# The V projection behind the G loop, and the PV matmuls of windowed attention one step later

## The reference

```
x1 = layernorm(x)
g = x1 @ Wg.T + bg ;  v = x1 @ Wv.T + bv          # 16 heads of 64
corr = g g^T / (|g_i| |g_j|), masked to j in [i-128, i]
corr = (corr + 1) / 2
denom = mean_j(corr) + 0.5
fit = 1 / (denom * sum_i(1 / denom))
attn = softmax_j(corr * fit, masked)
x = x + (attn @ v) @ Wo.T + bo
h = relu(layernorm(x) @ W_fc.T)^2 ; y = h @ W_proj.T
x = x + (spikes of y over 5 steps) / 5
```

## Time and profile before

| | us |
|---|---|
| median of 2 runs | 1728.33 (1723.23 to 1733.42) |
| the profiled execution | 1727.19 |
| its span on core 0, the slowest | 1726.2 |
| spans of the other cores | 1710.9 to 1723.3 |

### The profile page before, as it was taken

One profiled execution on the slowest core, in us unless ns is written; L12 is line 12 of the kernel. 1 busy time (PEld: TensorE's weight loads), 2 busy tenths in 40 slices (PEclk: granted clock), 3 DMA queues, 4 the chain that ended last, 5 costly groups with the idle time before them and its releaser, 6 DMA issues.

```text
span 1726.2 us, 16548 instructions; the slowest of 8 cores (1710.9 to 1726.2 us)
## 1 busy us (share of the span) xinstructions
PE 1063.4 (62%) x4632; PEld 436.4 (25%) x4632; DVE 680.6 (39%) x1639; ACT 672.6 (39%) x1467; POOL 132.5 (8%) x216
## 2 busy tenths in 40 slices
PE   0077675655355555555555787888688768877800
PEld 0022222222122222222222233333233323333300
DVE  1300002122455555555553203069505960394098
ACT  1333333333266666666665554045303540351000
POOL 1011111111000000000000010111011101111100
PEclk9976667778555555555555899999799989999955
DMA  9967665544100000000001344444444434445301
GB/s 186 223 122 131 121 90 87 106 110 104 44 1 1 1 1 1 1 1 1 1 1 54 118 135 144 125 145 147 158 123 135 154 142 143 125 156 156 112 19 54
DMA packets 78909, 158.71 MB, mean 92 GB/s; under 512 B 38627, under 2 KB 38884, under 8 KB 78820
## 3 DMA queue, kind: packets, MB, share of 16 engines
q0 software_dynamic: 63824, 106.97, 27.0%
q1 hardware_dynamic: 14996, 50.68, 8.8%
HBM read 147.15 MB, written 33.55 MB: 105 GB/s over the span
## 4 chain that ended last, share of the span: by engine, by line
DMA 29%; PE 25%; DVE 20%; issue 11%; ACT 8%; another core or an unknown queue 4%; POOL 1%; DVEq 1%; ACTq 0%; POOLq 0%; SPq 0%
PE psY L833 8%; DMA wpb<-wprojC 7%; DMA wstg<-wfcT 7%; DMA wstg<-wprojT 5%; ACT PT L584 4%; PE psY L795 4%; PE psPV L598 4%; DMA wfcC<-wstg 4%; DMA wfcb<-wfcC 4%; DVE memb L872 3%; DVE t1b L869 3%; DMA wprojC<-wstg 3%; PE psPT L575 3%; DVE accb L880 3%
## 5 line engine op out<-in xcount | busy, mean ns | idle before, releaser
L795 PE MATMUL psY<-x2nT,wfcb 128*128 128x512 bf16 x1024 | 236.1, 388 | 45.1 <-DMA wfcb<-wfcC 44.0
L833 PE MATMUL psY<-wpb,h_sb 128*128 128x512 bf16 x1024 | 237.0, 388 | 40.1 <-DMA wpb<-wprojC 39.0
L598 PE MATMUL psPV<-PT,v_sb 128*64 128x128 bf16 x512 | 103.8, 306 | 110.9 <-ACT PT L584 110.9
L481 DVE SCALAR_TENSOR_TENSOR C<-psD,maskA_sb 128x256 f32<-128x256 f32 x240 | 100.8, 420 | 153.1 <-PE psD L475 150.1
L524 ACT ACTIVATE ebf<-C,fit 128x256 f32<-128x256 f32 x256 | 151.4, 591 | 2.3 <-DVE em L563 0.6
L575 PE MATMUL psPT<-ident_sb,em 128*128 128x128 bf16 x512 | 97.8, 294 | 86.4 <-DVE em L563 84.7
L795 PEld LDWEIGHTS psY<-x2nT,wfcb 128*128 128x128 bf16 x1024 | 98.5, 99 | 182.0 <-issue 77.9
L833 PEld LDWEIGHTS psY<-wpb,h_sb 128*128 128x128 bf16 x1024 | 98.7, 99 | 177.1 <-issue 73.2
L352 DVE TENSOR_REDUCE rqv_sb<-gsq 128x16 f32<-128x1024 bf16 x16 | 19.5, 1220 | 296.6 <-ACT gsq L345 296.6
L851 ACT ACTIVATE y<-psY 128x512 f32<-128x512 f32 x32 | 16.1, 624 | 267.3 <-PE psY L833 267.3
L861 DVE TENSOR_SCALAR spkA<-y 128x1024 f32<-128x1024 f32 x16 | 11.1, 694 | 275.6 <-ACT y L851 274.3
(11 more groups left out here) (99 smaller groups left out, 1196.4 us busy)
## 6 DMA issues: line engine op xcount, KB each, us to landing
wfcb<-wfcC POOLq DMA_DIRECT2D x64, 512.0 KB, 4.1
wpb<-wprojC POOLq DMA_DIRECT2D x64, 512.0 KB, 3.9
xa<-xin SPq DMA_DIRECT2D x32, 512.0 KB, 4.4
wstg<-wfcT POOLq DMA_DIRECT2D x32, 256.0 KB, 6.8
xpair<-xin SPq DMA_DIRECT2D x8, 1024.0 KB, 12.2
wfcC<-wstg POOLq DMA_DIRECT2D x16, 512.0 KB, 3.4
wstg<-wprojT POOLq DMA_DIRECT2D x16, 512.0 KB, 5.6
wprojC<-wstg POOLq DMA_DIRECT2D x16, 512.0 KB, 2.9
```

The source lines that it names most:

```text
L481: msk=(mask0_sb if qt == 0 else maskA_sb): h.scalar_tensor_tensor(C_sb[hb][:, 256 * qt:256 * qt + 256], psD[qb][:], 1.0, msk[:], ALU.mult, ...
L598: mpv = b.op("T", lambda h, h_i=h_i, hp=hp, qt=qt, q4=q4, pb=pb, half=half: h.matmul(psPV[pb][hp:hp + 64, 128 * (q4 % 2):128 * (q4 % 2) + ...
L795: mmt = b.op("T", lambda h, f=f, fp=fp, k=k, gi=gi: h.matmul(psY[f % 2][:], wfcb[fp % 2][:, 1024 * (f % 2) + 128 * k:1024 * (f % 2) + 128 ...
L833: last = b.op("T", lambda h, f=f, f2=f2, tti=tti, nh=nh, pj=pj: h.matmul(psY[pj][:], h_sb[:, 512 * f + 128 * tti:512 * f + 128 * tti + 128 ...
```

## The change

Two edits. The V projection's loop over 16 row tiles leaves the x1T loop and runs as a loop of its own behind the G loop, with the same matmuls, evictions and waits. In the attention pipeline emit_pv takes block i-22 instead of i-21 and stands right behind emit_pass1 instead of last; the loop runs one iteration more.

```diff
@@ -273,8 +273,6 @@
-    psV_free = [None, None]
-    tok_v = None
     for t in range(NT):
@@ -302,20 +300,6 @@
-        for nh in range(2):
-            vi = (t * 2 + nh) % 2
-            mmt = None
-            for k in range(NC):
-                mmt = b.op("T", lambda h, vi=vi, tt=t, nh=nh, k=k: h.matmul(
...
-                    waits=[tok_wv, x1T_toks[t], psV_free[vi]])
-            ev = b.op("S", lambda h, vi=vi, tt=t, nh=nh: h.activation(
...
@@ -389,6 +373,24 @@
+    psV_free = [None, None]
+    tok_v = None
+    for tt in range(NT):
+        for nh in range(2):
+            vi = (tt * 2 + nh) % 2
+            mmt = None
+            for k in range(NC):
+                mmt = b.op("T", lambda h, vi=vi, tt=tt, nh=nh, k=k: h.matmul(
...
+                    waits=[tok_wv, x1T_toks[tt], psV_free[vi]])
+            ev = b.op("S", lambda h, vi=vi, tt=tt, nh=nh: h.activation(
...
@@ -617,9 +619,11 @@
-    for i in range(NSTEP + 22):
+    for i in range(NSTEP + 23):
         if i < NSTEP:
             emit_pass1(*hq(i))
+        if i >= 22 and i - 22 < NSTEP:
+            emit_pv(*hq(i - 22))
         if i >= 17 and i - 17 < NSTEP:
             emit_e(*hq(i - 17))
...
         if i >= 20 and i - 20 < NSTEP:
             emit_pt(*hq(i - 20))
-        if i >= 21 and i - 21 < NSTEP:
-            emit_pv(*hq(i - 21))
         if i < NSTEP and hq(i)[1] == NT - 1:
             emit_stats(hq(i)[0])
```

More of the change, by code:

```diff
@@ L304, in build_core @@
         tok_x1T = evs[-1]
-        for nh in range(2):
-            vi = (t * 2 + nh) % 2
-            mmt = None
-            for k in range(NC):
-                mmt = b.op("T", lambda h, vi=vi, tt=t, nh=nh, k=k: h.matmul(
-                    psV[vi][:], x1T[:, 2048 * k + 128 * tt:2048 * k + 128 * tt + 128],
-                    wvT_sb[:, 1024 * k + 512 * nh:1024 * k + 512 * nh + 512],
-                    start=(k == 0), stop=(k == NC - 1)),
-                    waits=[tok_wv, x1T_toks[t], psV_free[vi]])
-            ev = b.op("S", lambda h, vi=vi, tt=t, nh=nh: h.activation(
[L315 to L318, removed]
     psG_free = [None, None]
@@ L390, in build_core @@
         tok_g = evs[-1]
+    psV_free = [None, None]
[6 more added lines that the diff above has]
+                mmt = b.op("T", lambda h, vi=vi, tt=tt, nh=nh, k=k: h.matmul(
+                    psV[vi][:], x1T[:, 2048 * k + 128 * tt:2048 * k + 128 * tt + 128],
+                    wvT_sb[:, 1024 * k + 512 * nh:1024 * k + 512 * nh + 512],
+                    start=(k == 0), stop=(k == NC - 1)),
+                    waits=[tok_wv, x1T_toks[tt], psV_free[vi]])
+            ev = b.op("S", lambda h, vi=vi, tt=tt, nh=nh: h.activation(
+                v_sb[:, 1024 * (tt + 1) + 512 * nh:1024 * (tt + 1) + 512 * nh + 512],
+                psV[vi][:], AF.Identity), waits=[mmt, tok_vpad])
+            psV_free[vi] = ev
+            tok_v = ev
     def dump(name, src_sb, tok, width):
```

## The result

| | before | after |
|---|---|---|
| median, us | 1727.83 (10 runs, 1721.16 to 1735.96) | 1682.33 (11 runs, 1673.75 to 1690.76) |
| ratio, 95% interval | | 0.9737 [0.971, 0.9764] |
| profiled execution, span of the slowest core | 1726.2 (core 0) | 1677.1 (core 7) |
| spans of the other cores | 1710.9 to 1723.3 | 1652.6 to 1676.3 |

The change is worth 45 us. The forecast was 27 us, with a range that ended at 1684.

What follows compares the result with a forecast made beforehand. Core 0's weight-cache DMA chain was taken to bound attention's start, and queue order and latencies between engines its pace. 1727.2 + 0 (V behind G) - 27 (later PV) = 1700 us, 0.984; range 1684 to 1720.

Steps and rivals of the forecast that it cites:

- Part B: Attention: PV one iteration later and first after psD saves 27 us over 15 heads; stage falls to 463 us.
- Pairs: Attention, PV_odd to next PV_odd: 3.19 us in even heads, 3.45 in odd ones; a pair gains 0 or 0.21 us.
- the end of an odd head: Attention, three pairs around a head's statistics: 11.73 us in odd heads.
- D_even runs ahead: Attention, TensorE's queue: D_even is issued ahead of PV_even's wait for the PT eviction, its psD bank being free.
- Rival 2: Attention: a third chain holds every pair at 3.4 and half the head's end is won; 1717 us, chance 0.10.
- ScalarE's chain: Attention, PV_odd, its eviction, exp, PT eviction, PV_even, PV_odd: keeps its length, 3.45 us in odd heads, 3.19 in even.
- Part A: Projections: moving V behind G gains 0, some 27 us of TensorE's path being hidden behind core 0's weight cache.
- rival 3: Projections: TensorE ends them last and psD begins at 502, not 447.7; 1754 us, chance 0.04.
- the sum's shift of 0: Weight cache beside denser x loads: its end does not move, each load's bytes being equal; bounds -13 and +14 us.
- Rival 1: Projections: the weight cache's DMA chain is slowed by the dense x loads, +14 us; 1714 us, chance 0.12.
- Rival 5: Projections: the weight cache's DMA chain is relieved, -10 us or more; 1688 us, chance 0.08.
- rival 4: Attention: with PV packed against psD the granted clock leaves 0.50, saving some 51 us; 1650 us, chance 0.04.

Runs made afterwards that it cites:

- lag 24: Changed kernel with the PV matmuls two iterations later still (block i-24), same place: 1645.9 us, 0.9534 of the kernel before.
- the first two attempts to go further: Changed kernel with PV moved last in the iteration, 1693.75 us (0.9838); changed kernel with PV one iteration later, 1719.64 us (0.9972).
- B alone: Kernel before with only PV moved to block i-22 and behind emit_pass1, V left in the x1T loop: 1703.65 us, 0.9856.
- the chain freed: Kernel before with the weight cache's staging buffer where attention does not reuse it, so attention no longer waits for the cache: 1725.7 us, 1.0015.
- A alone: Kernel before with only the V projection moved behind the G loop, PV left in place: 1716.16 us, 0.9931.
- lag 23: Changed kernel with the PV matmuls one iteration later (block i-23), same place: 1719.64 us, 0.9972 of the kernel before.
- the last one: Changed kernel with lag 24, em ahead of the exponential and its row sums, and the cache's staging buffer out of attention's way: 1591.95 us, 0.9118.

## Why the prediction was right and wrong

**Part B, -27: right, in its mechanism and in every term.** Pairs 3.18 and 3.45 us (3.19 and 3.45 forecast); the end of an odd head 11.78 (11.73); the stage 464 us (463); alone it gave 25 us (18 to 32). The head's period, from the second to the last statistics instruction, is (851.28 - 455.14) / 14 = 28.3 us, 28.2 forecast. D_even runs ahead as said. Rival 2, that another chain holds the pair at 3.4, is out. But the prediction called ScalarE's chain the last one without listing the others; the one through em, which sets the pairs of lag 24 at 2.85 us, stood only 0.3 us behind it. That cost the forecast nothing here, but it misled the first two attempts to go further.

**Part A, 0: wrong. The step that failed** is "On core 0 the cache chain ends at 447 in any case, so the whole regrouping, some 27 us of TensorE's path, is hidden there and worth 0." The numbers were read rightly, but they are those of two cores. On the other six cores of that same trace the last write is at 399 to 410 and G, which ends at 429 to 437, holds psD; the prediction even says that on most others the projections bound. It then argued that the slowest core sets the time. But the slowest core is no fixed one (7 in the profile of after, 2 with B alone, 4 with the chain freed in the kernel before), and over 33 runs cores 0 and 1 were no later than the others. Freeing the chain changed nothing (1.0015), and in every kernel with part A its last write comes at 400 to 426 us, not at 444. The slow pace itself, about 13 us a step on cores 0 and 1, is real: it came in both traces of the kernel before. It came in none of the other kernels, not even in the one with part B alone, whose projections are the same line by line. Why is open. A core's wait counts for the maximum only if it makes that core the slowest in run after run.

What A really does: TensorE's path to attention ends at 388 to 400 us in place of 430 to 440, and the chain, at 404 to 424 in the kernels with A alone and with both parts, becomes the bound on all cores. The mean start over eight cores goes from 439.7 to 417.8 in the kernel with A alone, 22 us; its time fell by 12 us, 7 to 17. The remainder behind attention was 786.3 us on average in the profile of before and 793.8 in this one, 790.9 in that of after; it lay between 786 and 795 in all fourteen profiles. So why 22 us of earlier start are worth 12, and whether the earlier start makes the remainder longer, is open.

**The sizes inside A.** x1T loop: 62 us, 55 forecast. From the first x1n to the last it takes 57.6 / 15 = 3.84 us a tile. Tiles that wait for no load are 3.04 apart (2.94 by the earlier trace rows); the rest is 10.8 us of waiting for loads of x, 6.8 of them ahead of the fourth tile. G: 12.15 us a tile, 12.0 forecast. V: 58 us, not 77. The prediction scaled the stage's 114 us of busy time by the stage's mean clock of 0.68. But 10.3 of the 114 are transposes, and the mean clock is one over time, not over work. Core 0 of the kernel before, one tile: first the evictions, the normalising and the 8 transposes, then the 16 V matmuls.

```profile
131.70:135.30 3.60, 0.61 (x8) 0.46 (x8) 0.00 (x0) 2.81 (x4) 0.00 (x0) 0.89 1.09 93
135.35:141.90 6.55, 6.55 (x16) 2.14 (x16) 0.00 (x0) 0.60 (x1) 1.33 (x2) 0.54 0.41 153
```

The high clock fell into the stretch in which TensorE had next to nothing to do; the V matmuls ran at 0.54. The 103 us of V matmuls, scaled from 0.54 to the 0.96 of the new block, give 58. Together V's end is 395, 407 forecast. So rival 3 was never near.

**The chain beside the dense loads.** The writes of the cache on core 7 while x is loaded:

```profile
82.38 0.57 POOL L72 DMA_DIRECT2D wfcC<-wstg  x1 [75.73 <-DMA wstg<-wfcT]
...
101.05 0.56 POOL L72 DMA_DIRECT2D wfcC<-wstg  x1 [13.38 <-DMA wstg<-wfcT]
...
144.04 0.56 POOL L72 DMA_DIRECT2D wfcC<-wstg  x1 [4.81 <-DMA wstg<-wfcT]
155.24 0.57 POOL L72 DMA_DIRECT2D wfcC<-wstg  x1 [5.14 <-DMA wstg<-wfcT]
```

Four steps take 61.7 us, where four at the pace behind them (11.2 us) take 45: 17 us lost; on core 0, by the same sum, 14. Spread over the V stage of the kernel before, the same 8 MB cost core 2 about 11 (13 steps of 11.6 us, 10.8 behind them). So the sum's shift of 0, for equal bytes, holds to about 6 us. The chain's end says it more directly: the last write comes at 408 and 417 us on the mean of eight cores in the two other kernels with V in the x1T loop (the chain freed, B alone), and at 407 to 417 in the ten with A. Rival 1 (+14) is out. The Trainium skill's rule of turns between queues ("DMA: Bandwidth & Descriptors", Queues, rings and completion order), read as half pace through those 62 us, would have cost the chain 31 us; that is about twice the 14 to 17 that it lost.

**The total.** -25 (B, alone) and -12 (A, alone) make -37; both together gave -45. With the two intervals combined the sum lies between -29 and -45, and that of both together between -41 and -50, so that an interaction is neither shown nor excluded. Rival 5, "the cache chain is relieved" (1688), comes nearest by its number, and on cores 0 and 1 the last write did come 41 to 44 us earlier than in the profile of before. But the regrouping is not what relieved it, since the slow pace is gone with B alone too, and it was not the bound of a typical run before. That the number is near is luck.

**Signs.** Of those named, these came: the pair, the head's end, the stage of 463, D_even ahead, psD behind the last wprojC write with over 20 us of idle TensorE, the clock at 0.50. The one sign of error that came was the chain's end away from 447 by over 10 us.

## What to carry to other kernels

Before a wait on the slowest core is taken as the bound, look at the same wait on all cores, and at which core is the slowest over many runs. Here a chain held cores 0 and 1 in both traces, and freeing it gave nothing, since the other cores were as late by another cause. Before a busy time is scaled by a clock, take the clock in the rows of the matmuls themselves, not the mean of a stage with idle time in it.

In a software pipeline in which no engine is full, list all closed chains through the in-order queues, those too in which an instruction merely stands behind one that waits; a lag that shortens one chain can close another, and its parity against the other stages matters as much as its size. The cheapest edit is then to move an instruction whose inputs are long there ahead of one that waits: here em, which took 126 us from the stage of lag 23.

## What the runs showed of the hardware

- The same chain of loads and writes between DRAM and SBUF has two paces. Its last three wfcT steps take 12.6 to 13.0 us each on the mean on cores 0 and 1 in both traces of the kernel before, and 10.1 to 11.7 on the other cores there and on every core of the twelve other kernels. What sets it is open.
- Behind PV's eviction ScalarE starts the exp (128x256) 0.37 us after the eviction's start in even heads and 0.50 in odd ones, and the PT eviction 0.59 or 0.72 behind that. So pairs alternate between 3.18 and 3.45 us by the parity of the head. Heads of the two parities work in different halves of the partitions; that this is the cause was not tested.
- In the V stage of the kernel before the granted clock was 0.89 in a stretch with 0.61 us of TensorE's work in 3.60, and 0.54 in the 6.55 us of matmuls behind it.
- The granted clock of the attention stage stays at 0.50, TensorE's level of 1.2 GHz, in all versions: TensorE is busy for 278 of 464 us in the kernel after and for 273.5 of 373 in the last one. The Trainium skill ("TensorE: Matmul & The Clock Gate", What's actually happening) says that the half clock is the default and that activity releases it. The V block, with TensorE busy for 57.5 of 58 us, ran at 0.96, which agrees; in attention no version shows the release, so rival 4 did not come even with the shortest pairs.
